# A Mamba, feed-forward, attention and expert stack: x loaded first, dt*u spread by TensorE in the first pass, new orders of work

## The chip, the cores and the metric

One core of a Trainium2 chip runs the whole program in one launch. The metric is the device time of that launch in microseconds (us). The kernel before took 1990.47 us in the median of three runs (1987.96 to 1991.94).

## What is computed

The input x has 8 items of 512 tokens by 128 features, float32. Four layers follow, each `x = layernorm(x + layer(x))`:

```python
# layer 1: two Mamba branches, forward and backward in time
xi, z = split(x @ Win); u = silu(causal_conv4(xi))       # 256 channels
dt = softplus(u @ Wx[:, :8] @ Wdt + bdt); B, C = u @ Wx[:, 8:40]   # 16 states
h = exp(dt * A) * h + (dt * u) * B ;  y = sum_s(h * C) + u * D     # over 512 steps
out = (y * silu(z)) @ Wout                                # then norms, a relu block
# layer 2: silu(x w1) * (x w2), two gelu layers of 512, w3 (ternary weights)
# layer 3: causal attention, 8 heads, 2 latent key/value heads
# layer 4: 8 experts (silu(x w1) * (x w3)) @ w2, best two, weighted by softmax
```

## The kernel before

Features lie on the 128 partitions, the 512 tokens on the free axis. The scan of layer 1 is cut into 64 **units** an item: 2 branches (d) of 2 channel halves (the four halves are hf 0 to 3), each half in 16 units of 8 channels by 16 states. For each unit n

- SyncE loads `ring[n % 6]` (L549, 512 KB): dt and dt*u of 8 channels, each repeated over 16 partitions, out of `spread_dram`, where ScalarE's queue has stored `dd` (dt and dt*u of a half, L996, semaphore `kept`);
- ScalarE takes exp(dt*A) in place (`decay`, L950);
- VectorE multiplies dt*u by B into PSUM (`drive`, L1255; B lies in `ps_brow`) and scans (`scan`, L1263) into `hst`;
- GpSimd multiplies by C into `hc` (`read_out`, L1532);
- TensorE adds up the 16 states of four units (`reduce`, L633) into `ps_y`, which VectorE gates (`gate`, L1270, L1276).

The **head** (h) makes dt, u, z, B and C of a branch: x's transposes (xT, L660), products xi, z, x and dtp (L651), the convolution (L1307), SiLUs (L981, L984) and `dt_step` (L934 to L941, L1236 to L1245). **rest** (r) is the remainder of layers 1 to 3, **experts** (x) is layer 4. They run as a pipeline over items: while item b's units run, the rest of item b-1, the experts of item b-2 and the head of item b+1 are woven in. Each engine runs its instructions in order, and the strings in `ORDER` say, for each engine, which stream takes its next step (u, r, x, h, g; VectorE takes two u steps for a unit, a product and a scan). So there are a first pass (units of item 0, order `TURN_ORDER`), a second (without x), five in a hardware loop, one more, and then what is left of rest and experts. TensorE's results go to four PSUM banks g0 to g3, given out by `place` to the least recently used; a `claim` waits until the bank's last reader is done.

In the first pass TensorE also transposes the raw weights (stream t, `turn_weights`): 20 turns, two of A before the head, then w1, w2, four each of h1 and h2, w3, wq and so on. They use g0 and g1 and the heads of this pass g2 and g3; VectorE copies every turn out (`turned_out`, L1222, semaphore `w_cp`). SyncE first raises every semaphore of `PER` by a start value, then issues 20 loads (`w_in`), x of item 0, and 37 later loads (`w_later`), the experts' weights last.

## Time and profile before

| | us |
|---|---|
| median of 3 runs | 1990.47 (1987.96 to 1991.94) |
| the profiled execution | 1983.65 |
| its span | 1981.8 |
| busy: TensorE (matmul) | 1660.5 (84%) |
| busy: VectorE | 1547.1 (78%) |
| busy: ScalarE | 1120.8 (57%) |
| busy: GpSimd | 754.8 (38%) |

In the rows PE is TensorE's matmuls, PEld its weight loads, DVE VectorE, ACT ScalarE, POOL GpSimd, SP SyncE; SPq and ACTq are instructions that issue a DMA. L549 is line 549 of the kernel. PEclk is the granted clock of TensorE as a share of 2.4 GHz (0.50 is the level of 1.2 GHz). A time in brackets is how long the engine had stood idle before an instruction, with what ended the wait. Durations are from one profiled execution.

### The profile page before, as it was taken

What the parts mean: (1) busy time and instruction counts of PE and PEld (TensorE: products, weight loads), DVE (VectorE), ACT (ScalarE), POOL (GpSimd) and SP (SyncE); (2) the same over time, 40 slices, a digit from 0 to 9 for tenths busy, and PEclk for the clock granted to TensorE, in tenths of its full rate; (3) what the DMA queues carried; (4) which work ended last, traced back from release to release, by engine and by line L of the source; (5) the groups of instructions that cost most, each with busy time, mean ns of one, the idle gap of its engine ahead of it and who ended that gap; (6) DMA issues with size and microseconds to landing.
All of it is one profiled execution on the core that took longest, in us unless ns stands there. A gap on an engine that the chain in (4) does not pass through costs nothing.

```text
span 1981.8 us, 26962 instructions
## 1 busy us (share of the span) xinstructions
PE 1660.5 (84%) x8352; PEld 768.2 (39%) x8352; DVE 1547.1 (78%) x2173; ACT 1120.8 (57%) x1555; POOL 754.8 (38%) x601
## 2 busy tenths in 40 slices
PE   2434487889997999889997899889998999989988
PEld 0210123344443445344443345344443445434545
DVE  1999899869995899769995899869996999641404
ACT  2445387358744786458744786458744785433232
POOL 0345555324533355324533355324533445310102
PEclk8655699899999999899999999999999999989999
DMA  7999999657955687657955787657955686500000
GB/s 197 228 221 225 227 230 210 150 135 181 230 133 141 158 216 178 156 123 183 231 131 140 159 214 181 156 126 181 232 132 141 165 209 184 130 0 0 6 1 6
DMA packets 107915, 309.48 MB, mean 156 GB/s; under 512 B 15970, under 2 KB 32244, under 8 KB 107764
## 3 DMA queue, kind: packets, MB, share of 16 engines
q1 hardware_dynamic: 93556, 279.32, 59.5%
q10 hardware_dynamic: 14208, 28.32, 4.4%
q8 instruction: 74, 1.21, 0.3%
q14 instruction: 77, 0.63, 0.1%
HBM read 287.67 MB, written 19.92 MB: 155 GB/s over the span
## 4 chain that ended last, share of the span: by engine, by line
PE 36%; DVE 21%; ACT 21%; issue 12%; DMA 5%; ACTq 2%; DVEq 1%; SPq 1%; POOL 0%; POOLq 0%
PE ps_pair L698 8%; PE ps_pair L795 7%; DVE sb_hst L1263 7%; ACT L919 6%; PE ps_pair L854 5%; DMA sb_ring<-spread_dram 5%; PE ps_pair L783 4%; PE ps_pair L874 3%; PE ps_pair L651 3%; ACT sb_ring L950 3%; ACT sb_mix L1099 3%; DVE sb_dd L1241 2%; DVE ps_in L1255 2%; DVE sb_nmax L1404 2%; PE ps_pair L798 2%
## 5 line engine op out<-in xcount | busy, mean ns | idle before, releaser
L1532 POOL TENSOR_TENSOR sb_hc<-sb_hst,sb_crep 128x512 f32<-128x512 f32 x512 | 659.3, 1294 | 990.0 <-DVE sb_hst L1263 617.1
L1263 DVE TENSOR_TENSOR_SCAN sb_hst<-sb_ring,ps_in 128x512 f32<-128x512 f32 x512 | 620.5, 1212 | 21.2 <-ACT sb_ring L950 13.2
L950 ACT ACTIVATE sb_ring<-sb_ring,sb_A 128x512 f32<-128x512 f32 x512 | 345.2, 713 | 227.0 <-DMA sb_ring<-spread_dram 99.5
L1255 DVE TENSOR_TENSOR ps_in<-sb_ring,ps_brow 128x512 f32<-128x512 f32 x512 | 354.3, 692 | 22.1 <-DMA sb_ring<-spread_dram 4.7
L854 PE MATMUL ps_pair<-sb_mix,sb_ew 128*128 128x512 f32 x512 | 251.3, 625 | 19.8 <-ACT sb_h L1065 9.4
L919 ACT ACT_TABLE_LOAD x193 | 247.6, 1283 | 7.3 <-DVE sb_xd L1314 3.2
L633 PE MATMUL ps_y<-sb_hc,sb_const 128*32 128x512 f32 x1024 | 154.2, 677 | 83.0 <-POOL sb_hc L1532 59.4
L795 PE MATMUL ps_pair<-sb_g,sb_h 128*128 128x512 f32 x320 | 170.5, 658 | 23.4 <-DVE sb_dd L1243 11.1
L783 PE MATMUL ps_pair<-sb_h,sb_g 128*128 128x512 f32 (+3 forms) x512 | 165.4, 452 | 6.5 <-DVE sb_nmax L1404 3.2
L854 PEld LDWEIGHTS ps_pair<-sb_mix,sb_ew 128*128 128x128 f32 x512 | 96.0, 198 | 156.7 <-issue 87.1
L874 PEld LDWEIGHTS ps_pair<-sb_ew,sb_eh 128*128 128x128 f32 x1024 | 120.6, 192 | 37.3 <-issue 13.6
L874 PE MATMUL ps_pair<-sb_ew,sb_eh 128*128 128x128 f32 x1024 | 125.1, 277 | 8.9 <-DVE sb_eh L1472 5.3
L1565 POOL TENSOR_TENSOR sb_mix<-sb_mix 128x512 f32<-128x512 f32 x56 | 71.3, 1273 | 116.4 <-DVE sb_mix L1480 116.4
L698 PE MATMUL ps_pair<-sb_g,sb_h2T 128*128 128x512 f32 x256 | 113.8, 598 | 1.8 <-ACT sb_g L1065 1.8
L1404 DVE TENSOR_REDUCE sb_nmax<-ps_pair 128x2 f32<-128x256 f32 (+3 forms) x128 | 103.0, 814 | 15.7 <-PE ps_pair L786 15.3
L698 PE MATMUL ps_pair<-sb_h,sb_h1T 128*128 128x512 f32 x256 | 113.8, 598 | 0.0
L1099 ACT ACTIVATE sb_mix<-ps_pair 128x1024 f32<-128x1024 f32 x56 | 57.0, 1018 | 80.9 <-PE ps_pair L802 52.7
L1472 DVE TENSOR_TENSOR sb_eh<-ps_pair,sb_ea 128x512 f32<-128x512 f32 x128 | 82.5, 680 | 24.6 <-PE ps_pair L854 23.1
L783 PEld LDWEIGHTS ps_pair<-sb_h,sb_g 128*128 128x128 f32 x512 | 82.4, 190 | 47.6 <-issue 17.0
L795 PEld LDWEIGHTS ps_pair<-sb_g,sb_h 128*128 128x128 f32 x320 | 57.7, 201 | 103.9 <-issue 47.5
L1133 ACT ACTIVATE sb_ea<-ps_pair 128x512 f32<-128x512 f32 x128 | 71.0, 597 | 43.1 <-PE ps_pair L854 32.1
L1480 DVE TENSOR_TENSOR sb_mix<-ps_pair,sb_gates 128x512 f32<-128x512 f32 x64 | 43.6, 681 | 59.0 <-PE ps_pair L874 58.9
(219 smaller groups left out, 2037.9 us busy)
## 6 DMA issues: line engine op xcount, KB each, us to landing
sb_ring<-spread_dram SPq DMA_DIRECT2D x512, 512.0 KB, 5.6
spread_dram<-sb_dd ACTq DMA_DIRECT2D x32, 512.0 KB, 3.0
sb_brep<-cut_dram ACTq DMA_DIRECT2D x16, 256.0 KB, 3.8
sb_crep<-cut_dram ACTq DMA_DIRECT2D x16, 256.0 KB, 4.2
sb_xtok<-in_L_attn_x_dram SPq DMA_DIRECT2D x8, 256.0 KB, 5.1
sb_ew<-in_L_ffn_w_dram SPq DMA_DIRECT2D x2, 1024.0 KB, 8.5
out_dram<-sb_yy ACTq DMA_DIRECT2D x8, 256.0 KB, 2.3
sb_h<-in_L_ffn_h_w_dram SPq DMA_DIRECT2D x1, 1024.0 KB, 7.0
```

The lines of the kernel that those rows point to most:

```text
L633: ins = pe.matmul(ps_y[32 * q:32 * q + 32, :], red, hc[:, (4 * k + q) % 6, :], start=(j == 0), stop=(j == 3))
L698: ins = pe.matmul(o[:], l, r, start=(i == 0), stop=(i == len(lhs) - 1))
L783: pe.matmul(ps_pair[i % 2][:, k, 0:(t + 1) * P], qT[:, tl, r, :], kz[:, 2 * k + hf, 0:(t + 1) * P], start=True, stop=False)
L795: pe.matmul(ps_pair[0][:, hf, :], kz[:, 2 * k + hf, j * P:(j + 1) * P], qT[:, TILES[hf].index(t), :, :], start=True, stop=False)
L854: ins = pe.matmul(o[:], l, r, start=(i == 0), stop=(i == len(lhs) - 1))
L874: ins = pe.matmul(o[:, n * D:(n + 1) * D], eh[:, e % 2, c, n * P:(n + 1) * P], ew2[:, e, c, :], start=(c == 0), stop=(c == 1))
L919: act.preload_act_table_set(name)
L950: act.activation(ring[:, n % RING, 0, :], ring[:, n % RING, 0, :], ACT.Exp, scale=A[d][:, g:g + 1]).then_inc(sem["dA"], 1)
L1255: dve.tensor_tensor(ps_in[n % 2][:], ring[:, n % RING, 1, :], ps_brow[:], ALU.mult).then_inc(sem["dbu"], 1)
L1263: dve.tensor_tensor_scan(hst[:, HST_SLOT[n], :], ring[:, n % RING, 0, :], ps_in[n % 2][:], 0.0, ALU.mult, ALU.add).then_inc(sem["scan"], 1)
L1404: dve.tensor_reduce(nmax[:, tl, r, :, hf], ps_pair[i % 2][:, :, 0:(t + 1) * P], AX.X, ALU.max, negate=True).then_inc(sem["smax"], 1)
L1532: pool.tensor_tensor(hc[:, n % 6, :], hst[:, HST_SLOT[n], :], crep[n // NU][:], ALU.mult).then_inc(sem["hc"], 1)
```

## The change

- SyncE issues x first, then 12 loads of what the first head needs (the backward branch's vectors but alog are moved behind, 9 loads, `w_one`), then raises the semaphores, then 26 later loads. The experts' weights and the router's (11 loads, `w_experts`) are issued in the second pass, one behind every fourth unit.
- A new constant `sel` (0 and 1, 128x512) is loaded. In the first pass ScalarE copies dt*u of each half to `duk`, and TensorE spreads it: for each unit one product of a 32-row slice of `sel` with `duk` into one of g0 to g3 (stream d, 64 steps). VectorE's `drive` reads dt*u from that bank and B from SBUF; the ring loads of this pass bring dt alone, 256 KB.
- ScalarE copies the ten turns of w1, w2, h1 and h2 (`moved`); VectorE keeps the other ten (`turned`). Heads, turns and spreads of the first pass share all four banks.
- All order strings are new, `TURN_ORDER` and `ORDER`; each has the same steps as before, but for the t and d steps of the first pass.

```diff
+    for j in range(NJ):
+        c[:, C_SEL + j * P:C_SEL + (j + 1) * P] = p[:, None] % 32 == CU * j + p[None, :] % CU
...
+    turned=10, moved=10, spread=64, copied=4,
...
+    if name[:2] == "du":
+        return "dbu", int(name[2:]) + 1
+    if name[:4] == "turn":
+        i = int(name[4:])
+        return ("moved", i - 1) if 2 <= i < 12 else ("turned", i + 1 if i < 2 else i - 9)
...
     DVE=(
-        "uxuxuuxuxxguuuuxuuuuuxrxuxurruxuuurxuhuruuuuuxxuururuhuhuruxuuxrruuhuuruuxuuuuhhrguuuuruuuuuuxuuuuuuhuuuruuuuu"
-        "ruuruxuguxuuruuxrrhruxuxuuhuhrxrhuxuruxururuhrruurrurxrrxrrurrururrhuhuuuhuruuuruurghhruuuuuuuuuururruuuuruurr"
-        "uurruhruur"),
+        "urxxuxuuxuxguuxxuuuuuuuuxxurxuuuxrurxuhurhxuuuuuurhuruuuuhrxuuuxruuururuuruuxuuhguururruuruuuuhxuuuuuhuuuuuuuu"
+        "uuhuuxhuuruugruuruxruxuxuxuhrxrhxuurxurruhrururrrurururrrxrrxrrhhuuuhrurruuuuhuruhruuuuuuuuuurrrhuuuruguuuurru"
+        "uuuruuruur"),
...
 TURN_ORDER = dict(
     PE=(
-        "ththhtutthttutuutthhhhttuthtutttuhtuuhuhhhhhuuhhuutuu"),
+        "tddddtddtuddudddtdttduhdutdddhhddtddtduddhthdudtddhdduddhddduhdhdduhtdddudtdtdhuddtdhudhdhtddddtdtduddddhutddh"
+        "ddhduuh"),
...
     DVE=(
-        "uthuuuuutuuuutuuuuthuhuthtuuuuuutuuuutuuuutguuuutuuhugtuthuuuuhuuhtuttuuuuuuutuuuhuuuuutuuuuuutuuuuuuuuuuguuhu"
-        "uuuhuuuuuuuhhuuuhuuuuuuhhuuuuuuuuuguuuhuuuuuuhuuuuuuuuuuuu"),
+        "ttuuuutuuuuuuuttuuutuuututuuuuuuuuhuutuuguuuhuhuutuuuuhuuguuuuuuhuuuhutuuuuuuuuuuuuuuhuuuuuuuuuuthguuuutuuuuuu"
+        "uhtuhhuuuhtuuuuuuhutuuuuuuutuuguthuuuuuuuuuuhuuuuhuuuuhuhu"),
...
 NONE = {f"g{i}": None for i in range(4)}
-PROLOGUE, _after = place(section("h" * len(ZERO), [(step, 0) for step in ZERO]), NONE, PAIRS[1])
-FIRST, _after = place(section(TURN_ORDER["PE"]), _after, PAIRS[1])
+PROLOGUE, _after = place(section("tt" + "h" * len(ZERO), [(step, 0) for step in ZERO], TURNS), NONE)
+FIRST, _after = place(section(TURN_ORDER["PE"]), _after)
 SECOND, _after = place(section(without(ORDER["PE"], "x")), later(_after))
...
+        sel = xn[:].rearrange("p (j n) -> p j n", j=NJ)
+        duk = ea[:, 2:4, :]
...
+        MOVED = ("w1", "w2", "h1", "h2")
...
-        M_LOADS, R_LOADS = 20, 37
+        M_LOADS, ONE_LOADS, R_LOADS, EXPERT_LOADS = 12, 9, 26, 3 + E
...
-            loads = [(const[:], a["const"][:, 0:C_MASK]), (mask, a["const"][:, C_MASK:C_END])]
+            loads = [(const[:], a["const"][:, 0:C_MASK])]
+            loads += [(alog[d], a[f"{pre}_Alog"].rearrange("(g c) s -> g (c s)", c=CU)) for d, pre in enumerate(("fw", "bw"))]
+            ones = [(mask, a["const"][:, C_MASK:C_SEL])]
             for d, pre in enumerate(("fw", "bw")):
-                loads += [
+                (loads, ones)[d].extend([
                     (winx[d][:], a[f"{pre}_Win"][:, 0:DI]),
                     (taps[d][:], a[f"{pre}_convw"].rearrange("(h p) k -> p h k", p=P)),
                     (winz[d][:], a[f"{pre}_Win"][:, DI:2 * DI]),
                     (wx[d][:], a[f"{pre}_Wx"].rearrange("(h p) k -> p h k", p=P)),
+                    *((cols[d][:, i, :], a[f"{pre}_{v}"].rearrange("(h p) -> p h", p=P))
+                      for i, v in enumerate(("convb", "D"))),
                     (wdt[64 * d:64 * d + R, :], a[f"{pre}_Wdt"]),
-                    (wdt[64 * d + R + 2 * S:64 * d + R + 2 * S + 1, :], a[f"{pre}_bdt"].rearrange("(o c) -> o c", o=1)),
-                    (alog[d], a[f"{pre}_Alog"].rearrange("(g c) s -> g (c s)", c=CU))]
-                loads += [(cols[d][:, i, :], a[f"{pre}_{v}"].rearrange("(h p) -> p h", p=P))
-                          for i, v in enumerate(("convb", "D"))]
-            assert len(loads) == M_LOADS, len(loads)
+                    (wdt[64 * d + R + 2 * S:64 * d + R + 2 * S + 1, :], a[f"{pre}_bdt"].rearrange("(o c) -> o c", o=1))])
+            loads += [(sel, a["const"][:, C_SEL:C_END].rearrange("p (j n) -> p j n", j=NJ))]
+            assert len(loads) == M_LOADS and len(ones) == ONE_LOADS, (len(loads), len(ones))
             later = [(wout[d][:], a[f"{pre}_Wout"].rearrange("(h p) n -> p h n", p=P))
...
-            assert len(later) == R_LOADS, len(later)
-            for name in PER:
-                sp.sem_inc(sem[name], first(name))
+            later += [(s3, a["w3_s"].partition_broadcast(P))]
+            experts = [(ew1[:], a["ew1"].rearrange("e p h -> p e h")),
+                       (ew3[:], a["ew3"].rearrange("e p h -> p e h")), (wgate[:], a["w_gate"])]
+            experts += [(ew2[:, e, :, :], a["ew2"][e].rearrange("(c p) n -> p c n", p=P)) for e in range(E)]
+            assert len(later) == R_LOADS and len(experts) == EXPERT_LOADS, (len(later), len(experts))
             with nc.allow_non_contiguous_dma(reason="per-channel vectors, once"):
+                sp.dma_start(xtok[:], a["x"][0:1].rearrange("o (n p) d -> p (o n) d", p=P)).then_inc(sem["x_in"], 16)
+                for dst, src in loads[:-3]:
+                    sp.dma_start(dst, src).then_inc(w_in, 16)
                 sp.wait_ge(w_zero, 1)
-                for dst, src in loads:
+                for dst, src in loads[-3:]:
                     sp.dma_start(dst, src).then_inc(w_in, 16)
-                sp.dma_start(xtok[:], a["x"][0:1].rearrange("o (n p) d -> p (o n) d", p=P)).then_inc(sem["x_in"], 16)
+                for name in PER:
+                    sp.sem_inc(sem[name], first(name))
+                for dst, src in ones:
+                    sp.dma_start(dst, src).then_inc(w_one, 16)
                 for dst, src in later:
                     sp.dma_start(dst, src).then_inc(w_later, 16)
 
-            def sequence(at, nxt, x_next=None):
+            def sequence(at, nxt, x_next=None, half=False, experts=()):
...
                     rows = spread[hf, 32 * q + CU * j:32 * q + CU * (j + 1), :]
-                    sp.dma_start(ring[:, n % RING, :, :].rearrange("p a t -> p (a t)"),
-                                 rows.unsqueeze(0).broadcast_to([S, CU, 2 * T])
-                                 ).then_inc(sem[f"ring{n % RING}"], 16)
+                    if half:
+                        sp.dma_start(ring[:, n % RING, 0, :], rows[:, 0:T].unsqueeze(0).broadcast_to([S, CU, T])
+                                     ).then_inc(sem[f"ring{n % RING}"], 16)
+                    else:
+                        sp.dma_start(ring[:, n % RING, :, :].rearrange("p a t -> p (a t)"),
+                                     rows.unsqueeze(0).broadcast_to([S, CU, 2 * T])
+                                     ).then_inc(sem[f"ring{n % RING}"], 16)
 
                 for n in range(UNITS):
                     load(at(0), n)
+                    if n % 4 == 3:
+                        for dst, src in itertools.islice(more, 1):
+                            sp.dma_start(dst, src).then_inc(w_experts, 16)
                     if n == 2 and nxt:
                         sp.wait_ge(sem["full_h"], at(0)("full_h", HEAD_INDEX["xT"] + 1))
                         sp.dma_start(xtok[:], x_next.rearrange("o (n p) d -> p (o n) d", p=P)).then_inc(sem["x_in"], 16)
 
-            sequence(counts(0), True, a["x"][1:2])
-            sequence(counts(1), True, a["x"][2:3])
...
-            def turn_weights():
+            def turn_weights(tabs):
                 for i, (kind, c) in enumerate(TURNED):
-                  o = turn_banks[i % 2]
+                  o = claim_of(counts(0), tabs[i >= 2])(f"turn{i}")
                   if i == 2:
                       pe.wait_ge(w_later, 16 * R_LOADS)
-                  if i >= 2:
-                      pe.wait_ge(w_cp, i - 1)
+                      pe.wait_ge(sem["turned"], 2 + first("turned"))
+                  if i == 12:
+                      pe.wait_ge(sem["moved"], 10 + first("moved"))
...
                 ins.then_inc(sem["y_red"], 1)
+
+            def spreads(at, tab):
+                row, claim = at(0), claim_of(at, tab)
+                for n in range(UNITS):
+                    hf, j, q = n // 16, n % 16 // 4, n % 4
+                    o = claim(f"du{n}")
+                    pe.wait_ge(sem["copied"], row("copied", hf + 1))
+                    rows = slice(32 * q, 32 * q + 32)
+                    pe.matmul(o[:], sel[rows, j, :], duk[rows, hf % 2, :], start=True, stop=True).then_inc(sem["spread"], 1)
+                    yield
 
...
+            pe.wait_ge(w_set, 1)
+            at, turning = counts(0), turn_weights((PROLOGUE, FIRST))
             next(turning)
             next(turning)
             alone(head(at, 0, 0, PROLOGUE))
-            interleave(TURN_ORDER["PE"], dict(u=units(at, False), t=turning, h=heads(at, FIRST)))
+            pe.wait_ge(w_one, 16 * ONE_LOADS)
+            interleave(TURN_ORDER["PE"], dict(u=units(at, False), d=spreads(at, FIRST), t=turning, h=heads(at, FIRST)))
             at = counts(1)
+            pe.wait_ge(w_mask, 1)
...
 
+            def turned_out():
+                for i, (kind, c) in enumerate(TURNED):
+                    if kind in MOVED:
+                        dst = dict(w1=w1T[:], w2=w2T[:], h1=h1T[:, c, :], h2=h2T[:, c, :])[kind]
+                        act.wait_ge(w_tp, i + 1)
+                        act.activation(dst, bank[FIRST[f"turn{i}"][0][0]][:], ACT.Copy).then_inc(sem["moved"], 1)
+                    if i >= 2:
+                        yield
...
+                    if keep:
+                        act.wait_ge(sem["spread"], row("spread", 16 * hf - 16 if hf >= 2 else 0))
+                        act.activation(duk[:, hf % 2, :], dd[:, 1, :], ACT.Copy).then_inc(sem["copied"], 1)
...
             at = counts(0)
-            alone(head(at, 0, 0, PROLOGUE))
-            interleave(TURN_ORDER["ACT"], dict(u=units(at), h=heads(at, FIRST, False)))
+            alone(head(at, 0, 0, PROLOGUE, keep=True))
+            act.wait_ge(w_one, 16 * ONE_LOADS)
+            interleave(TURN_ORDER["ACT"], dict(u=units(at), t=turned_out(), h=heads(at, FIRST, False, keep=True)))
             at = counts(1)
...
+            dve.memset(vertex[:], -0.75 * THIRD).then_inc(w_const, 1)
             dve.wait_ge(w_in, 16 * M_LOADS)
             dve.tensor_copy(identb[:], ident)
-            dve.tensor_copy(maskb[:], mask)
-            dve.tensor_copy(pick[:], const[:, C_PICK:C_PICK + 2 * KV]).then_inc(w_set, 1)
+            dve.tensor_copy(pick[:], const[:, C_PICK:C_PICK + 2 * KV])
 
...
+                    if kind in MOVED:
+                        yield
+                        continue
...
 
-            def drive(row, n):
+            def drive(row, n, tab=None):
                 if n % NU == 0:
                     dve.wait_ge(sem["brep"], row("brep", 16 * (n // NU + 1)))
                     dve.wait_ge(sem["dbu"], row("dbu", n))
-                    dve.tensor_copy(ps_brow[:], brep[:]).then_inc(sem["brow"], 1)
+                    dve.tensor_copy(eh[:, 1, 0, :] if tab else ps_brow[:], brep[:]).then_inc(sem["brow"], 1)
                     dve.wait_ge(sem["brow"], row("brow", n // NU + 1))
+                brow = eh[:, 1, 0, :] if tab else ps_brow[:]
                 dve.wait_ge(sem["scan"], row("scan", n - 1))
-                dve.wait_ge(sem[f"ring{n % RING}"], row(f"ring{n % RING}", 16 * (n // RING + 1)))
-                dve.tensor_tensor(ps_in[n % 2][:], ring[:, n % RING, 1, :], ps_brow[:], ALU.mult
-                                  ).then_inc(sem["dbu"], 1)
+                if tab:
+                    dve.wait_ge(sem["spread"], row("spread", n + 1))
+                    du = bank[tab[f"du{n}"][0][0]][:]
+                else:
+                    dve.wait_ge(sem[f"ring{n % RING}"], row(f"ring{n % RING}", 16 * (n // RING + 1)))
+                    du = ring[:, n % RING, 1, :]
...
             next(turning)
             alone(head(at, 0, 0, PROLOGUE))
-            interleave(TURN_ORDER["DVE"], dict(u=units(at, False), g=gates_of(at, False), t=turning, h=heads(at, FIRST)))
+            dve.wait_ge(w_one, 16 * ONE_LOADS)
+            dve.tensor_copy(maskb[:], mask).then_inc(w_mask, 1)
+            interleave(TURN_ORDER["DVE"], dict(u=units(at, False, FIRST), g=gates_of(at, False), t=turning, h=heads(at, FIRST)))
```

## Rows read from the trace of the kernel before

**Rows 1.** Busy times of the start and of passes (windows, us from the start).

```profile
core 0: us, PE busy (x) PEld busy (x) DVE busy (x) ACT busy (x) POOL busy (x), PEclk, DMA share, GB/s
0.00:55.66 55.66, 15.58 (x29) 6.07 (x30) 11.30 (x27) 15.29 (x22) 1.97 (x9) 0.82 0.73 201
55.66:221.56 165.90, 68.02 (x245) 22.77 (x243) 159.15 (x214) 69.88 (x102) 79.65 (x62) 0.56 0.93 224
221.56:425.25 203.69, 163.05 (x828) 67.35 (x828) 170.40 (x214) 119.56 (x167) 86.08 (x67) 0.92 0.79 188
...
648.10:871.85 223.75, 203.15 (x1031) 94.17 (x1030) 190.63 (x265) 142.82 (x197) 94.07 (x74) 0.97 0.70 168
```

**Rows 2.** Instructions in order of time, first loads to x's transposes (start, us, engine, line).

```profile
5.83 2.05 SPq L528 DMA_DIRECT2D sb_const<-in_const_dram  x1
...
15.91 0.46 SPq L528 DMA_DIRECT2D sb_cols<-in_L_attn_bw_D_dram  x1
16.42 0.47 SPq L529 DMA_DIRECT2D sb_xtok<-in_L_attn_x_dram  x1
...
18.04 0.23 DVE L1176 CAST sb_identb<-sb_const 128x128 bf16<-128x128 f32 x1 [17.07 <-DMA sb_cols<-in_L_attn_bw_D_dram]
...
19.50 1.11 PE L660 MATMUL ps_pair<-sb_const,sb_xtok 128*128 128x128 f32 x4 [0.37 <-DMA sb_xtok<-in_L_attn_x_dram]
```

**Rows 3.** The first head in order of time, and the page's row of the stores.

```profile
25.99 1.28 ACT L919 ACT_TABLE_LOAD   x1
26.00 3.37 DVE L1307 SCALAR_TENSOR_TENSOR sb_u<-ps_pair,sb_taps,sb_u 128x511 f32<-128x511 f32 x5 [0.90 <-ACT sb_u L975]
...
28.77 3.58 PE L651 MATMUL ps_pair<-sb_xT,sb_winz 128*128 128x512 f32 x4 [3.62 <-DVE sb_u L1307]
...
32.89 1.14 ACT L984 ACTIVATE sb_u<-sb_u 128x512 f32<-128x512 f32 x2
...
44.13 0.35 ACTq L996 DMA_DIRECT2D spread_dram<-sb_dd  x1
...
50.16 0.60 ACT L934 ACTIVATE sb_dd<-ps_pair 128x512 f32<-128x512 f32 x1 [8.40 <-DMA spread_dram<-sb_dd]
...
55.05 0.69 DVE L1245 TENSOR_TENSOR sb_dd<-sb_dd,sb_u 128x512 f32<-128x512 f32 x1
...
spread_dram<-sb_dd ACTq DMA_DIRECT2D x32, 512.0 KB, 3.0
```

**Rows 4.** VectorE in the first pass, one turn's copy between units, in order of time.

```profile
73.91 0.67 DVE L1222 COPY sb_h1T<-ps_pair 128x512 f32<-128x512 f32 x1
74.49 0.69 DVE L1255 TENSOR_TENSOR ps_in<-sb_ring,ps_brow 128x512 f32<-128x512 f32 x1
...
76.33 0.69 DVE L1255 TENSOR_TENSOR ps_in<-sb_ring,ps_brow 128x512 f32<-128x512 f32 x1
```

**Rows 5.** Waits of ScalarE in the first pass; VectorE's first late ring load.

```profile
ACT sb_ring L950 <- DMA sb_ring<-spread_dram: 55.4, 35, 3.5
...
222.93 0.69 DVE L1255 TENSOR_TENSOR ps_in<-sb_ring,ps_brow 128x512 f32<-128x512 f32 x1 [0.69 <-DMA sb_ring<-spread_dram]
```

**Rows 6.** One loop pass: VectorE's longest waits (648.1 to 871.9 us), and a window.

```profile
DVE sb_g L1415 <- ACT sb_rstd L1107: 7.9, 1, 7.9
...
DVE sb_yy L1415 <- ACT sb_rstd L1107: 6.5, 1, 6.5
...
720.00:732.00 12.00, 11.61 (x38) 3.92 (x36) 11.58 (x15) 7.72 (x9) 6.00 (x6) 1.00 0.87 234
```

**Rows 7.** TensorE: two products in each of two rows; windows (us, busy, PEclk, DMA share, GB/s).

```profile
21.38 3.78 PE L651 MATMUL ps_pair<-sb_xT,sb_winx 128*128 128x512 f32 x4 [0.77 <-ACT sb_xT L968]
...
679.59 1.88 PE L651 MATMUL ps_pair<-sb_xT,sb_winx 128*128 128x512 f32 x4
...
235.00:240.00 5.00, 4.18 (x9) 0.82 1.03 229
...
255.00:260.00 5.00, 2.55 (x6) 1.00 0.70 176
```

More of the change, by code:

```diff
@@ L176, with section @@
 PER["full"], PER["full_e"] = len(REST_INDEX), len(EXP_INDEX)
+TURNS = [[f"turn{i}"] for i in range(20)] + [[]]
+SPREADS = [[f"du{n}"] for n in range(UNITS)]
 CHAIN = [(step, 0) for step in ONE + [[]]] + [(step, 1) for step in ZERO]
-def section(order, heads=CHAIN):
-    steps = dict(r=iter([(step, -1) for step in REST]), x=iter([(step, -2) for step in EXPERTS]), h=iter(heads))
+def section(order, heads=CHAIN, turns=TURNS[2:]):
+    steps = dict(d=iter([(step, 0) for step in SPREADS]), t=iter([(step, 0) for step in turns]), r=iter([(step, -1) for step in REST]), x=iter([(step, -2) for step in EXPERTS]), h=iter(heads))
     uses = []
@@ L446, in two_layer_kernel @@
         block = ctx.enter_context(nc.Block())
-        turn_banks = [bank[f"g{i}"] for i in range(2)]
         def first(name):
@@ L539, in count @@
                     return value
+                more = iter(experts)
                 def load(row, n):
@@ L557, in sequence @@
                         sp.dma_start(xtok[:], x_next.rearrange("o (n p) d -> p (o n) d", p=P)).then_inc(sem["x_in"], 16)
[L559 to L560 removed]
+            sequence(counts(0), True, a["x"][1:2], half=True)
+            sequence(counts(1), True, a["x"][2:3], experts=experts)
             with sp.Fori(0, B - 3) as b:
@@ L956, in units, with head @@
                     yield
-            def head(at, ahead, d, tab, prev=True):
+            def head(at, ahead, d, tab, prev=True, keep=False):
                 row = at(ahead)
@@ L1003, in head, with heads @@
                     yield
-            def heads(at, tab, prev=True, nxt=True):
-                yield from head(at, 0, 1, tab, prev)
+            def heads(at, tab, prev=True, nxt=True, keep=False):
+                yield from head(at, 0, 1, tab, prev, keep)
                 if prev:
@@ L1189, in turned_out @@
                 for i, (kind, c) in enumerate(TURNED):
-                    o = turn_banks[i % 2]
+                    o = bank[(PROLOGUE, FIRST)[i >= 2][f"turn{i}"][0][0]]
                     if i == 2:
```

52 lines of the change are left out of this document (25 added, 27 removed).

## The prediction

> **What bounds the kernel now.** I read the busy times of each pass first [rows 1], then the start of the run in order of time [rows 2, 3], then the first pass by engine [rows 4, 5], and last one pass of the loop [rows 6]. A pass is one item's 64 units. The reader is to see four stretches: 55.7 us up to the first unit, 165.9 us for the first pass, 203.7 us for the second, then about 223 us a pass [rows 1]. In the first pass VectorE is the bound: busy 159.2 of 165.9 us, TensorE only 68.0, at a granted clock of 0.56 (mostly the 1.2 GHz level). ScalarE waits there for ring loads (55.4 us in all [rows 5]), but VectorE itself has hardly any wait, so that those loads are in time for it; from 222.9 us on they no longer are: VectorE waits eight times for a ring load, 4.6 us in all (the first is in [rows 5]). In the loop VectorE is busy 190.6 of 223.8 us and TensorE 203.2 [rows 1]; both are nearly full until the attention rounds, in which VectorE waits 7.9 and 6.5 us for the normaliser [rows 6].
>
> The profiled execution took 1983.65 us (span 1981.8), the median of three runs is 1990.47: the sum goes against 1983.65, and 6.8 us are put on top.
>
> **Start.** SyncE raises 78 semaphores up to 5.83 us, and 20 loads go out before x [rows 2]; other engines start at about 0.8. After the change the loads go first: 2.05 us for the first, 12 more at 0.46, so the last (sel, 256 KB) is issued at about 8 us. x, of the same size, was there 3.1 us after its issue (16.42 to 19.50 [rows 2]), so the weights are in at 11.0 us; from there to x's transposes the two A turns take 1.1 us (18.04 to 19.12). Transposes at 12.1 instead of 19.50: **-7.4 us**. The increments end at about 13.5, before the semaphores are asked for that come late in the list, or cost under 1 us.
>
> The first head now has four banks. Before, z00 waited for the bank of xi00 until 28.77, so the SiLUs of z ended at 33.0 and those of u came behind them, at 32.89 to 34.03 [rows 3]. With a bank of its own z follows xi at 25.2 [rows 7], z01 is there at 28.9, ScalarE is through with it at 29.5 and with u at 30.7 (its table load ends at 27.3, the convolution at 29.4 [rows 3]): **-3.3 us**.
>
> The store of dt and dt*u took 5.96 us (44.13 to 50.1 [rows 3]), beside 7.8 MB of weights; the median of such stores is 3.0 [rows 3]. It now starts at 33.4, with 4.5 MB queued and no experts' weights behind. I take 5.0, with 3.0 and 6.0 as ends: **-1.0 us**. The second half's dt*u then ends at 44.0 instead of 55.74 [rows 3]. The 26 later loads are issued from 18 to 36 us (18.4 us before), so they are in by 39; VectorE's preparation of them (57.0 to 61.2) comes behind 44.0 and does not wait.
>
> **First pass, VectorE.** A unit costs it 1.84 us (74.49 to 76.33 [rows 4]), 118 for 64. The ten copies of w1, w2, h1, h2 go: 0.67 us each, but the next product starts 0.59 us after such a copy [rows 4], so 10 x 0.59 = 5.9; the mask's cast (0.2) comes in: **-5.7 us**. The product has one operand in PSUM and one in SBUF before and after, so it stays at 0.69.
>
> **First pass, added work.** ScalarE gets ten copies and four of dt*u at 0.60 us (as its copy of xT), 8.4 us; it is busy 69.9 of 165.9 us, so they are hidden while decays stand ahead of need. Its earliest turn copy holds a bank that du3 needs; it comes after three decays, at about 48 us, and du3 is needed at 51. TensorE gets 64 products of 32 rows by 512 columns. The nearest rows are its products of 128 and 41 rows: 1.89 us each at the 1.2 GHz level, 0.90 at 2.4 [rows 7]. So 121 or 58 us beside its 68.0 (at a clock of 0.56). Cold it would want 189 us, more than VectorE's 153.5; but where it was busy 4.18 of 5 us the clock went up, and it stayed up with 2.55 busy of 5 [rows 7]. With the products it will be busy 55 to 65% in short gaps. I take the high clock for most of the pass. What can be late: a spread product can run only three banks ahead, shared with turns and heads, and behind it in TensorE's queue stand y's reductions, each of which waits for GpSimd. For VectorE that adds between 0 and 25 us of waits; I take **+5** (nearer to nothing, since before the change VectorE stands idle 6.7 us of this pass, with a TensorE that runs cold and is as often in wait behind y's reductions [rows 1]).
>
> The Trainium skill ("TensorE: Matmul & The Clock Gate", section "A second HAM failure mode: psum-queue depth-cycling") speaks against the change: a TensorE that cycles through PSUM banks with small idles between its groups is throttled and released again and again. By it the pass would come out as in the second case below.
>
> **Ring loads.** Halved in the first pass: 256 KB against 1.85 us is 142 GB/s, where 512 KB a unit were 283, above the 229 GB/s that the queues moved when saturated [rows 7]. The ring is then full at the second pass, and the 4.6 us of waits there go. In their place come 2 MB of experts' weights behind units 3 and 7 of the second pass: 1 MB at 229 GB/s is 4.6 us each, 9 us against a cushion of about 6 units less the 0.4 us by which each full load falls behind. I put 4.6 of it as wait: net **0**, ends -4.6 and +5.
>
> **The new orders of all later passes.** This edit has no row of its own. Counted in the strings of VectorE: before, 53 of 64 units and all gates stand ahead of the dt step that frees the banks of the attention rounds; after it 51 units, and the last gate behind. That moves two units (3.7 us) and a gate (0.73 + 0.69) into the stretch where VectorE waits 14.4 us [rows 6]. If VectorE alone set the time before it, a pass would gain 5.1 us. TensorE was just as full there (in one stretch of 12 us it was busy 11.61 and VectorE 11.58 [rows 6]), so most will not pass. Against it, some steps may now be late by up to 2 us. Between -5.1 and +2 I take -1.5 for each of six passes: **-9 us**.
>
> **Sum.** -7.4 - 3.3 - 1.0 - 5.7 + 5 + 0 - 9 = -21.4: 1962.2 for a profiled execution, **1969** in the median.
>
> **The rivals.**
> 1. Forecast, within about 9 us of 1969: 0.47.
> 2. Slower: TensorE stays at 1.2 GHz in the first pass and becomes its bound. 189 us instead of 153.5 + 5: 30.5 us more, 1999.6. At the high clock its work is about 95 us, so it decides from a share f of low clock at which 189f + 95(1-f) passes 153.5, f = 0.62, and eats all of the 21.4 from 0.91. For it: the clock of 0.56 now. Against: the rise in [rows 7]. 0.08. This is the case of the page named above.
> 3. TensorE's queue order, not its clock, holds the spread products up: 20 us of waits instead of 5, 1984. 0.12.
> 4. The orders gain nothing and cost 2 us a pass: +12 instead of -9, 1990, no change: 0.10. With 3 us, +18: 1996, slower: 0.08.
> 5. The moved units pay nearly in full, -4.5 a pass, -27: 1951. For it: 14.4 us of wait to fill. 0.15.
>
> **How the numbers follow.** A measurement can tell about 0.2%, 4 us. Cases 1, 3 and 5 are faster, 0.74; the first half of case 4 is the same, 0.10; case 2 and the rest of 4 are slower, 0.16. The range leaves out the slower cases, 0.16, and the far end of case 5: 1947 to 1993. The likeliest case alone: 1960 to 1978.
>
> **What the changed profile would show.** x's transposes at about 12 us, VectorE's first unit near 49 with its second head's dt*u ended at 44; TensorE's clock in the first pass over 0.8 and no long waits of ps_in for its spread product; the second pass starting near 205 instead of 221.6; ring loads late after unit 4 of the second pass; passes of 218 to 223 us, with shorter waits for the normaliser. The prediction is wrong if the passes move by over 3 us either way, if the spread products queue behind the reductions, or if the sel load or late increments hold up the first head.

## The result, and the profile after

The changed kernel took 2008.6 us in the median (2008.1 to 2009.5) against 1989.2 for the kernel before on the same chips: a ratio of 1.0096, 95% interval 1.0079 to 1.0114. It is slower by about 19 us; the forecast was 1969, with a range of 1947 to 1993. The profiled execution has a span of 2006.4 against 1981.8.

Windows of the changed kernel, cut like [rows 1] (columns as there):

```profile
0.00:45.67 45.67, 17.17 (x33) 6.42 (x34) 15.12 (x41) 19.20 (x29) 1.97 (x9) 0.76 0.76 199
45.67:214.20 168.53, 141.75 (x368) 42.87 (x366) 150.10 (x188) 73.24 (x112) 80.04 (x62) 0.58 0.37 118
214.20:423.29 209.09, 166.63 (x828) 68.76 (x828) 170.45 (x215) 118.60 (x165) 84.80 (x67) 0.90 0.82 196
650.72:876.25 225.53, 203.91 (x1033) 94.93 (x1033) 190.92 (x266) 142.38 (x196) 93.40 (x74) 0.96 0.69 167
```

Cut at the first copy of B of each pass, the difference of the spans is accounted for like this:

| stretch | before | after | difference | forecast |
|---|---|---|---|---|
| start and first pass, to the second pass | 221.6 | 214.2 | -7.4 | -12.4 |
| second pass | 203.7 | 209.1 | +5.4 | -1.5 |
| five passes of the loop | 1110.1 | 1127.4 | +17.3 | -7.5 |
| the last pass and what is left | 446.5 | 455.7 | +9.2 | 0 |
| sum | 1981.8 | 2006.4 | +24.6 | -21.4 |

So the stretch up to the second pass still gains, and everything behind it loses. Two signs stand in the rows. In the first pass TensorE has twice the work and is still at the 1.2 GHz level (clock 0.58). In the loop the busy times are those of before [rows 1], and the pass shown is 1.8 us longer (the five together 17.3): it waits, it does not work more. The table compares two single profiled executions; that of before was 5.6 us under the median, so 24.6 us here stand beside 19 in the medians.

The waits of VectorE in one loop pass (line that waited, for what: us in total, times, longest). Before, 871.85 to 1094.24:

```profile
DVE sb_g L1415 <- ACT sb_rstd L1107: 7.9, 1, 7.9
DVE sb_yy L1415 <- ACT sb_rstd L1107: 6.4, 1, 6.4
...
DVE sb_nmax L1404 <- PE ps_pair L786: 1.2, 4, 0.3
...
DVE sb_hst L1263 <- POOL sb_hc L1532: 0.3, 1, 0.3
...
DVE sb_hst L1263 <- issue: 0.2, 1, 0.2
```

After, 876.25 to 1101.34:

```profile
...
DVE sb_yy L1478 <- ACT sb_rstd L1163: 7.3, 1, 7.3
DVE sb_hst L1326 <- issue: 3.3, 3, 1.8
DVE sb_nmax L1467 <- PE ps_pair L827: 2.6, 6, 0.9
DVE sb_hst L1326 <- POOL sb_hc L1598: 2.1, 1, 2.1
DVE sb_g L1478 <- ACT sb_rstd L1163: 1.6, 1, 1.6
```

The reader is to see that the waits for the normaliser did shrink as forecast, 14.3 to 8.9 us, and that scans now have longer waits that the profile puts down to nothing (`issue`, 3.3 instead of 0.2), scans wait for GpSimd (2.1 instead of 0.3) and maxima for TensorE (2.6 instead of 1.2). The rows below show that the longest of the `issue` waits is one for a decay.

Where the longest new wait of a scan comes from, in order of time, VectorE first, then ScalarE, in the changed kernel:

```profile
724.08 0.69 DVE L1303 TENSOR_TENSOR sb_dd<-sb_dd,sb_u 128x512 f32<-128x512 f32 x1
...
726.17 0.69 DVE L1319 TENSOR_TENSOR ps_in<-sb_ring,ps_brow 128x512 f32<-128x512 f32 x1
728.70 1.22 DVE L1326 TENSOR_TENSOR_SCAN sb_hst<-sb_ring,ps_in 128x512 f32<-128x512 f32 x1 [1.84 <-issue]
```

```profile
724.80 0.35 ACTq L1049 DMA_DIRECT2D spread_dram<-sb_dd  x1
725.34 0.57 ACTq L1056 DMA_DIRECT2D sb_brep<-cut_dram  x1
726.01 0.55 ACTq L1058 DMA_DIRECT2D sb_crep<-cut_dram  x1
726.60 1.28 ACT L963 ACT_TABLE_LOAD   x1 [2.98 <-issue]
727.89 2.56 ACT L994 ACTIVATE sb_ring<-sb_ring,sb_A 128x512 f32<-128x512 f32 x4
```

ScalarE's string has here the step `keep2` (it waits for the third half's dt*u, stores it, and loads B and C). It stands behind 22 decays; in the string of before it stands behind 24. VectorE makes that dt*u at the same point as before (its last product starts 73.4 us into the pass; 73.5 before). ScalarE therefore stands in `keep2` until 724.8, issues three DMAs, loads a table, and only then makes the decay for which the next scan waits. In the kernel before the same place has the three issues, but two decays more in hand and no table load between the issues and the next decay, and the scan does not wait:

```profile
722.32 0.35 ACTq L996 DMA_DIRECT2D spread_dram<-sb_dd  x1
...
723.69 0.69 DVE L1255 TENSOR_TENSOR ps_in<-sb_ring,ps_brow 128x512 f32<-128x512 f32 x1
724.28 1.21 DVE L1263 TENSOR_TENSOR_SCAN sb_hst<-sb_ring,ps_in 128x512 f32<-128x512 f32 x1
```

### The profile page after: what moved, and what is told of

It reads as the page before. It is cut to its first block, busy times and chain, and to the rows that moved or that the text cites. A ratio compares the mean times of both kernels' runs of the same rounds, so it can differ in the third digit from the quotient of the medians.

```text
span 2006.4 us, 27294 instructions
## 1 busy us (share of the span) xinstructions
PE 1756.6 (88%) x8480; PEld 798.6 (40%) x8480; DVE 1543.0 (77%) x2163; ACT 1126.8 (56%) x1565; POOL 750.8 (37%) x601
## 4 chain that ended last, share of the span: by engine, by line
PE 54%; ACT 15%; DVE 15%; issue 9%; POOL 3%; DMA 2%; ACTq 1%; DVEq 0%; SPq 0%; POOLq 0%
PE ps_pair L739 12%; PE ps_pair L895 8%; PE ps_pair L836 7%; PE ps_pair L824 6%; PE ps_pair L692 5%; PE ps_pair L915 5%; DVE sb_hst L1326 4%; PE ps_y L664 3%; ACT L963 3%; ACT sb_mix L1155 2%; POOL sb_hc L1598 2%; PE ps_pair L675 2%; PE ps_pair L839 2%; ACT sb_ring L994 2%; DMA sb_ring<-spread_dram 2%
## 5 line engine op out<-in xcount | busy, mean ns | idle before, releaser
L1326 DVE TENSOR_TENSOR_SCAN sb_hst<-sb_ring,ps_in 128x512 f32<-128x512 f32 x512 | 620.8, 1213 | 53.0 <-issue 21.4
L1319 DVE TENSOR_TENSOR ps_in<-sb_ring,ps_brow 128x512 f32<-128x512 f32 x448 | 310.6, 693 | 27.1 <-DMA sb_ring<-spread_dram 9.3
L895 PE MATMUL ps_pair<-sb_mix,sb_ew 128*128 128x512 f32 x512 | 260.7, 644 | 6.0 <-DVE sb_g L1415 2.1
L739 PE MATMUL ps_pair<-sb_g,sb_h2T 128*128 128x512 f32 x256 | 120.6, 622 | 0.0
L675 PE MATMUL ps_pair<-sb_ea,sb_xn 32*128 32x512 f32 x128 | 77.4, 1021 | 13.4 <-DVE sb_dd L1301 4.9
```

The lines of the kernel that those rows point to most:

```text
L675: pe.matmul(o[:], sel[rows, j, :], duk[rows, hf % 2, :], start=True, stop=True).then_inc(sem["spread"], 1)
L739: ins = pe.matmul(o[:], l, r, start=(i == 0), stop=(i == len(lhs) - 1))
L895: ins = pe.matmul(o[:], l, r, start=(i == 0), stop=(i == len(lhs) - 1))
L1319: dve.tensor_tensor(ps_in[n % 2][:], du, brow, ALU.mult).then_inc(sem["dbu"], 1)
L1326: dve.tensor_tensor_scan(hst[:, HST_SLOT[n], :], ring[:, n % RING, 0, :], ps_in[n % 2][:], 0.0, ALU.mult, ALU.add).then_inc(sem["scan"], 1)
```

## The experiments

Each was timed beside the kernel before; the ratio is to that. All compute the same as the kernel before except e5, whose text says what differs.

| run | edit | median us | ratio | 95% interval |
|---|---|---|---|---|
| e1 | changed kernel, old `ORDER` | 1983.4 | 0.9967 | 0.9948 to 0.9987 |
| e2 | kernel before, new `ORDER` | 2014.1 | 1.0126 | 1.0080 to 1.0172 |
| e4 | e1 without spreads | 1976.1 | 0.9929 | 0.9905 to 0.9953 |
| e5 | e1, spreads over 128 rows | 1975.2 | 0.9917 | 0.9885 to 0.9949 |
| e6 | e1, experts' loads in first pass | 1976.0 | 0.9941 | 0.9919 to 0.9962 |
| e7 | e5 made exact, with e6 | 1967.3 | 0.9901 | 0.9874 to 0.9927 |
| e8 | before, new ScalarE string alone | 2086.5 | 1.0511 | 1.0475 to 1.0548 |
| e9 | before, the other three new | 2079.9 | 1.0470 | 1.0451 to 1.0489 |
| e10 | changed kernel, keep2 two decays later | 1989.8 | 1.0016 | 1.0000 to 1.0031 |
| e11 | e10, GpSimd's old string | 1987.6 | 0.9988 | 0.9971 to 1.0006 |
| e12 | e4 with e6 | 1976.9 | 0.9951 | 0.9936 to 0.9966 |
| e13 | e1, keep2 two decays earlier | 1994.2 | 1.0041 | 1.0028 to 1.0055 |

**The orders against the rest: e1 and e2.** e1 puts the strings of `ORDER` of before into the changed kernel, e2 the new ones into the kernel before; `TURN_ORDER` stays as it is in each.

> The changed kernel with the ORDER strings of before (TURN_ORDER stays new). Theory A, the new strings cost the loss: five loop passes took 1127.4 us in the changed kernel against 1110.1, the last pass and the end 455.7 against 446.5, so about 26 us come back: 1982 us, loop passes of about 222.7. Theory B, something else makes the later passes longer (the banks' state handed over, the experts' loads, other addresses): 2008 us, passes of 225.5.

> The kernel before with the new ORDER strings alone. Theory A: 1989 + 26 = 2015 us, loop passes of about 225.5. Theory B: 1989 us, passes of 222.7. If the two edits act together only, e1 and e2 both stand near 1989.

Theory A holds. The same strings cost 25.2 us in one kernel (2008.6 against 1983.4) and about 25 in the other (ratio 1.0126, a wide interval of 16 to 34 us). In e1 the five loop passes take 1106.7 us and the end 446.4, before's or a little under. The second pass is no longer by the strings (210.0 in e1, 209.1 in the changed kernel): they cost 4.1 us a pass of the loop in the mean and 9 in the last pass and the end. The slowdown is the strings; all the rest of the change together gains 0.3%.

**Which step of the strings: e8, e9, e10, e13.** e8 gives the kernel before ScalarE's new string alone, e9 the three others.

> The kernel before, with only ScalarE's string of the later passes new. All new strings together cost it 25 us (e2: 2014.1), 2.7 us in each pass of the loop (225.1 against 222.4). Theory H: ScalarE's string does most of it, because it puts the step that waits for dt*u and issues the store (keep2) behind 22 decays instead of 24, while VectorE reaches that dt*u at the same unit as before; decays then come late: 224 to 225.5 us a pass and 2000 to 2014 us in all. Rival I: the loss comes from TensorE's or VectorE's string and ScalarE's alone is harmless: passes of 222 to 223 us and 1987 to 1992.

> The kernel before with the new strings of TensorE, VectorE and GpSimd, and its own old string of ScalarE; e2, with all four new, took 2014.1, and e8, with ScalarE's alone, 2086.5 (237 us a pass, the strings no longer fit each other). e10 showed that one letter of ScalarE's string is worth 19 us in the changed kernel. Theory K: ScalarE's old string, which has keep2 behind 24 decays, cures that loss here too, at 224 us a pass: 1990 to 1998. Rival L: the old string is as far from the other three new ones as in e8 and the passes run to 230 us or more: above 2020. If the three new strings are as good as I forecast (1.5 us a pass gained), it would be under 1985.

Both came out near 2080, 237 and about 235 us for a pass of the loop. e8 lies far above both of its theories; in it VectorE's scans wait 21.4 us for decays in one pass. e9 came out as its rival L had said. Each engine's string fits the other three; split, neither half can be priced, and the two runs don't say which step of the strings costs the time. e10 leaves the strings together and moves one letter of ScalarE's, `keep2`, the sixth `h` of the line:

```diff
-        "xuxxuxuxuxuuxxruruxruhuuruuxrxxhhrruuuuxruhrurruruhurhuuruxuxxruxuurhuuruuruxuuruxuuuhhxruxhrhurrxhurrxruruurh"
+        "xuxxuxuxuxuuxxruruxruhuuruuxrxxhhrruuuuxruhrurruruhuruuhruxuxxruxuurhuuruuruxuuruxuuuhhxruxhrhurrxhurrxruruurh"
```

> The changed kernel with one letter of ScalarE's string moved: keep2 (the copy and store behind the wait for dt*u) after 24 decays instead of 22, all else new. In the changed kernel VectorE's scan then waits 1.84 us for the decay behind it (728.70 us). Theory H in its narrow form (this one step is the loss): passes of 223 to 224 us instead of 225.2, seven of them: 1997 to 2001 us against 2008.6. Rival J: the 1.84 us are only where the delay shows; ScalarE and GpSimd are late in other places as well (decays behind 29 and 40, GpSimd's adds), so the pass gains under 0.6 us: 2004 to 2009.

18.8 us came back by the medians (2008.6 to 1989.8), 16 by the ratios (1.0096 to 1.0016): two thirds to three quarters of the 25, and more than theory H had said. Half a pass of the loop (first copy of B to the second) fell from 99.0 us to 97.1, before's length. ScalarE in e10 at this place:

```profile
722.00 1.28 ACT L963 ACT_TABLE_LOAD   x1
723.17 0.35 ACTq L1049 DMA_DIRECT2D spread_dram<-sb_dd  x1
723.29 0.72 ACT L994 ACTIVATE sb_ring<-sb_ring,sb_A 128x512 f32<-128x512 f32 x1
```

The table is loaded before the wait, and a decay starts 0.12 us behind the store's issue. VectorE's waits marked `issue` at scans fall from 3.3 to 1.4 us a pass; those for the normaliser, for GpSimd and of the maxima stay as in the changed kernel:

```profile
DVE sb_hst L1326 <- issue: 1.4, 2, 1.2
```

The five loop passes take 1116.9 us (1127.4 with the step early) and the end 448.4 (455.7). In the changed kernel the wait of 1.84 us stands in every one of the passes two to eight (1.84 to 1.94, 13.0 us in all); in e10 it stands in none. Of the 18.4 us between the two spans, 13.8 lie in the first halves of these passes, where the step stands. The rest lies elsewhere, and it is not even: in the third and fourth pass of the loop the second half gave the gain back (225.0 and 224.6 us in e10, 225.1 and 224.9 in the changed kernel). e13 is the reverse test, with all old strings (the fifth and sixth `h`; the step ahead of `keep2` has to go with it):

```diff
-        "uxxxxxuxuuuuxurruxuuxruhrxuurxuxhrruuxuhhxurruuruuruuhxhruururrxxuuuhruuuuruururxhhuxxxuuurhruhrurrrxxxuhuxrrr"
+        "uxxxxxuxuuuuxurruxuuxruhrxuurxuxhrruuxuhhxurruuruuhhruuxruururrxxuuuhruuuuruururxhhuxxxuuurhruhrurrrxxxuhuxrrr"
```

> e1 (all old strings, 1983.4) with two letters of ScalarE's string moved: dt2 and keep2 behind 22 decays instead of 24, everything else old. It asks whether the place of keep2 costs the time by itself, without the other new strings. Theory H: VectorE reaches this dt*u at its unit 23, as before, so ScalarE stands in keep2 until then, decay 22 comes late, and VectorE's scan waits 1.5 to 3 us in each of seven passes: passes of 224 to 225.5 instead of 222.3, 1994 to 2006 in all. Rival R: keep2's place matters only with the other new strings, whose units leave VectorE no cover; then the passes stay within 0.7 us and the run at 1981 to 1988.

Against e1, ratio to ratio, it costs 0.74%, 15 us. Half a pass grows from 97.1 to 98.4 us, the five passes from 1106.7 to 1118.2; the first halves of the seven passes hold 10.2 of the 16.7 us between the spans. ScalarE stands still for 8.4 us and the scan behind it is late (ScalarE, then VectorE):

```profile
953.46 2.56 ACT L994 ACTIVATE sb_ring<-sb_ring,sb_A 128x512 f32<-128x512 f32 x4 [8.39 <-issue]
```

```profile
954.27 1.22 DVE L1326 TENSOR_TENSOR_SCAN sb_hst<-sb_ring,ps_in 128x512 f32<-128x512 f32 x1 [0.64 <-DVE ps_in L1319]
```

The profile puts that wait down to the product, which had ended at 953.63; the first of the four decays begun at 953.46 ended about 0.5 us later (an estimate, a quarter of 2.56 us).

So the place of this one step costs 15 to 19 us in either set of strings: theory H holds, with both signs of the edit. A quarter (e10) and four tenths (e13) of the difference between the spans lie outside the halves in which the step stands, and how they come about was not traced.

**What is left of the strings' cost: e11.** It is e10 with GpSimd's string of before.

> e10 (the changed kernel with keep2 two decays later, 1989.8) with GpSimd's old string. What is left of the new orders' cost against e1 (1983.4) is 6.4 us. In each pass of e10 VectorE waits 2.1 us once for GpSimd's product (its scan at 1076.06 us), where the kernel before waits 0.3. Theory M: GpSimd's new string, with its adds in other places, is the cause: passes 1 to 2 us shorter, 1976 to 1986. Rival N: that wait is the shadow of something on TensorE's or VectorE's side, and the passes stay at 225: 1987 to 1993; if the old adds come where they hold up a product of the new order, above 1993.

The wait of 2.1 us for GpSimd's product is still there, and the five loop passes take 1116.2 us against 1116.9 in e10: theory M, 1 to 2 us a pass, falls. The median is 2 us under e10's and the two intervals overlap, so a small gain is not excluded. What e10 and e11 stand above e1, 6 and 4 us by the medians, 10 and 4 by the ratios, stays unexplained. Two places were seen and not tested. Behind the middle of a pass a scan waits 1.24 us for a decay that stands behind two table loads of ScalarE (in e10 the scan at 984.29, the loads at 979.78 and 982.18). It does so in six passes of e10, 7.4 us in all, and of e11; in e1 the waits of scans marked `issue` come to 2.4 us in the whole run. The difference of 5.0 us has the size of what is left, but no run moves those steps. And TensorE holds more of the chain that ended last. Its shares by engine in e10, then in e1 (before: PE 36%):

```profile
PE 55%; ACT 15%; DVE 14%; issue 9%; POOL 3%; DMA 2%; SPq 2%; ACTq 1%; DVEq 0%; POOLq 0%
```

```profile
PE 39%; DVE 21%; ACT 20%; issue 13%; DMA 4%; ACTq 2%; DVEq 1%; SPq 0%; POOL 0%; POOLq 0%
```

That share is a weak sign: e13, with TensorE's old string, has 48%. No run separates TensorE's string from VectorE's.

**The first pass: e4, e5.** e4 takes the spread products, their copies and the halved loads out again. e5 keeps them and lets each product run over all 128 rows instead of 32; dt*u of the first item is then a sum over four rows, another number than the reference's, and the loads, decays and instruction counts are the same.

```diff
-                    rows = slice(32 * q, 32 * q + 32)
+                    rows = slice(0, P)
```

> As e1, but without TensorE's spread products, duk copies and halved ring loads: the first pass loads dt*u with the ring as before; early loads, four banks and ScalarE's copies of the turns stay. Theory C, the 32-row products at the low clock cost VectorE its gain (18.4 us of idle time in the first pass against 6.7 before): the first pass shrinks from 168.5 to about 160 us, 1974 us. Theory D, the idle time comes from the weave of heads and turns in TURN_ORDER, not from the products: 168 us, 1982 us.

> As e1, but each spread product takes all 128 rows of sel and duk instead of 32 (so it adds up four channel groups and dt*u is another number; the rest is computed as before). The instruction count and columns are the same. Theory E, the clock stayed at the 1.2 GHz level through stretches of 5.00 of 5 us busy because only 32 rows of the array worked: the granted clock of the first pass goes from 0.58 to over 0.8, products take about 0.9 us, VectorE's waits for them go, 5 to 8 us faster than e1. Theory F, the rows do not matter: clock 0.58, same time as e1.

Windows of the first pass: e1, e4, e5.

```profile
45.95:214.47 168.52, 141.88 (x368) 42.86 (x366) 150.09 (x189) 73.41 (x112) 79.97 (x62) 0.58 0.39 119
```

```profile
45.74:207.63 161.89, 64.53 (x238) 21.72 (x238) 148.78 (x188) 75.24 (x113) 79.72 (x62) 0.61 0.96 230
```

```profile
46.01:205.44 159.43, 117.16 (x368) 38.75 (x366) 150.09 (x188) 73.47 (x112) 80.04 (x62) 0.87 0.41 125
```

Theories C and E hold. With 32 rows the pass takes 168.5 us, 6.6 more than without spreads at all; with 128 rows the same 368 instructions run at a clock of 0.87 and it takes 159.4. VectorE stands idle for 18.4 us of the pass in e1 and for 9.3 in e5. Only a part of that is the wait for the spread product itself: 4.2 us in six waits in e1 and in the changed kernel, 1.7 us in e5. The rest is spread over other waits: 3.9 us of the convolution's step for ScalarE (1.3 in e5), 2.5 of a scan for GpSimd (the same in e5) and smaller ones. That TensorE was not idle in the slow case shows in the changed kernel:

```profile
95.00:100.00 5.00, 5.00 (x11) 1.71 (x8) 4.91 (x7) 2.44 (x5) 3.73 (x4) 0.50 0.38 107
100.00:105.00 5.00, 5.00 (x12) 0.70 (x10) 4.03 (x7) 4.10 (x7) 1.94 (x2) 0.50 0.42 106
```

By the records it is busy in every microsecond from 90 to 120 us, and at the 1.2 GHz level throughout; the ends of products are modelled, so this says only that its records leave no gap.

**The second pass: e6.** The experts' 11 loads move into the first pass, whose queues are two thirds empty (DMA share 0.37).

```diff
-            sequence(counts(0), True, a["x"][1:2], half=True)
-            sequence(counts(1), True, a["x"][2:3], experts=experts)
+            sequence(counts(0), True, a["x"][1:2], half=True, experts=experts)
+            sequence(counts(1), True, a["x"][2:3])
```

> Same as e1 (changed kernel with the old order of the later passes), but the experts' 11 loads are issued in the first pass, behind every fourth unit, and none in the second. In e1 the second pass took 210.0 us (214.5 to 424.4) against 203.7 of the kernel before. Theory F: the two loads of 1 MB behind units 3 and 7 of the second pass make its ring late and cost it about 6 us; then the second pass here takes 203 to 206 us, and the run is 4 to 7 us under e1's 1983.4: 1976 to 1979. The DMA share of the first pass was 0.37 in e1, so that 4 MB more there cost nothing. Rival G: the second pass is longer because its start finds less work ahead (the first pass leaves VectorE without lead); then it stays at 209 to 211 us and the run at 1982 to 1985. If the loads now disturb the first pass (168.5 us in e1), it gets longer by up to 4 us.

The second pass took 202.6 us instead of 210.0, the first 2.0 more. Theory F holds. VectorE's waits for ring loads in it were 9.3 us in the changed kernel and 7.1 in e1, and 1.5 in e6. Two of those in the changed kernel stand behind the two loads of 1 MB (in order of time):

```profile
229.28 0.70 DVE L1319 TENSOR_TENSOR ps_in<-sb_ring,ps_brow 128x512 f32<-128x512 f32 x1 [4.51 <-DMA sb_ring<-spread_dram]
...
242.17 0.70 DVE L1319 TENSOR_TENSOR ps_in<-sb_ring,ps_brow 128x512 f32<-128x512 f32 x1 [2.62 <-DMA sb_ring<-spread_dram]
```

**A version that beats both: e7, and what the spreads are worth: e12.** e7 makes e5 exact. Sixteen 0/1 matrices of 128x128, zero outside the unit's 32 rows, lie in the room of the experts' first weights until those are loaded, behind unit 15 of the second pass; the other experts' loads go into the first pass.

```diff
+    for q in range(4):
+        for j in range(NJ):
+            s = C_SEL + (4 * q + j) * P
+            c[:, s:s + P] = p[:, None] == 32 * q + CU * j + p[None, :] % CU
...
-                    rows = slice(32 * q, 32 * q + 32)
-                    pe.matmul(o[:], sel[rows, j, :], duk[rows, hf % 2, :], start=True, stop=True).then_inc(sem["spread"], 1)
+                    pe.matmul(o[:], sel[:, 4 * q + j, :], duk[:, hf % 2, :], start=True, stop=True).then_inc(sem["spread"], 1)
```

> e1 with each spread as a product of all 128 rows: sixteen 0/1 matrices of 128x128, zero outside the 32 rows of the unit's channels, in the room of the experts' first weights; those are loaded late in the second pass (behind unit 15), the others in the first pass. What is computed is the same. In e5, where 128 rows worked but summed a wrong dt*u, the granted clock of the first pass rose from 0.59 and 0.57 to 0.93 and 0.82 and the pass took 159.4 us instead of 168.5. Theory E (the clock goes by how many rows work) with theory F (the two big loads early in the second pass cost 6 us): first pass 159 to 161 us, clock above 0.8, second pass 203 to 206 us, the run 1966 to 1971. If zeros in most rows count as not working, the clock stays near 0.58, the first pass takes 168, and the run 1975 to 1979. If F is wrong, it is 1973 to 1976 with the high clock. The 1 MB selection load comes before the second unit and may delay the first ones by up to 4 us.

> e4 (old orders, no spread products, full ring loads in the first pass) with the experts' loads in the first pass as in e6. It prices what the spreads make room for. In e4 the first pass took 161.9 us at a DMA share of 1.00 and 0.92, so there is no room: 4 MB at the 229 GB/s of full queues are 18 us. Theory P: VectorE then waits for ring loads, the first pass grows by 10 to 18 us to 172 to 180, the second shrinks by 6 to 7 to 204: 1979 to 1988. Rival Q: the ring of six units and the slower start give enough cover, and the first pass grows by under 5 us: 1969 to 1975, as good as e7 (1967.3), and then the spread products bring nothing.

e7's first and second pass, then e12's first:

```profile
45.19:206.76 161.57, 116.97 (x371) 39.43 (x369) 149.86 (x189) 74.51 (x114) 79.71 (x62) 0.88 0.47 140
206.76:409.86 203.10, 162.34 (x823) 67.48 (x828) 170.36 (x215) 118.63 (x166) 85.39 (x67) 0.93 0.79 191
```

```profile
45.75:215.37 169.62, 64.67 (x238) 21.68 (x238) 148.99 (x188) 74.35 (x111) 79.72 (x62) 0.60 0.97 236
```

e7 takes 1967.3 us, 1.0% less than before. Most of the 128 rows meet zeros here, and the granted clock is that of e5 (0.88). e12 lies between its two theories: full queues cost the first pass 7.7 us (VectorE's waits for ring loads rise from 5.2 to 10.1), not 10 to 18, and the run is 9.6 us behind e7. With the clock up and the room in the queues unused the spreads bring nothing that can be measured (e5 1975.2, e4 1976.1). So they do pay, once the clock is up and something else uses the room that they leave in the queues.

## Why the prediction was wrong

**The orders were the largest miss.** In the profiled executions 46 us lie between the forecast of -21.4 and the measured +24.6. 34.0 of them are in the five loop passes, the last pass and the end, where the only term was "Between -5.1 and +2 I take -1.5 for each of six passes". The other 12 came up to the end of the second pass, from the first pass and the ring loads. The terms follow in the order of the sum.

**Start: right, and a little under.** Two instructions of the changed kernel's start, in order of time:

```profile
0.76 0.46 SPq L541 DMA_DIRECT2D sb_xtok<-in_L_attn_x_dram  x1
...
10.26 1.11 PE L701 MATMUL ps_pair<-sb_const,sb_xtok 128*128 128x128 f32 x4
```

x's transposes came at 10.26 us (forecast 12.1); the first issue took 0.46 us, not the 2.05 that I had carried over from [rows 2]. The store took 3.4 us, not 5.0, and the second dt*u ended at 41.42, not 44.0: -14.3 instead of -11.7. The first unit began only 10.0 us earlier, because VectorE's preparation of the later loads now stands ahead of it (the mask's cast up to the copy of B, 4.3 us); before it stood behind the first product. Before, then after:

```profile
55.66 0.69 DVE L1251 COPY ps_brow<-sb_brep 128x512 f32<-128x512 f32 x1
...
56.98 0.29 DVE L1194 COPY sb_wkrep<-sb_wkd 128x64 f32<-128x64 f32 x2
```

```profile
41.34 0.22 DVE L1569 CAST sb_maskb<-sb_eh 128x128 bf16<-128x128 f32 x1
...
45.67 0.43 DVE L1309 COPY sb_eh<-sb_brep 128x512 f32<-128x512 f32 x1
```

**First pass: the place of the error was named, its size not.** VectorE fell to 150.1 us busy; with the 4.3 us that moved ahead of the pass that is 154.4, where 153.5 were forecast. But it stood idle for 18.4 us (6.7 before); the term of +5 was about 12. The step that failed is "I take the high clock for most of the pass": the granted clock was 0.58. It read the clock by the busy share in [rows 7], from products that were nearly all of 128 rows, and applied it to products of 32. e5 and e7 show that at the same instruction count the pass has 0.58 with 32 rows and 0.87 and 0.88 with 128. With the clock up, in e5, VectorE's idle time is 2.6 us over that of before, inside what the term allowed. The second rival's clock was right, its price not: TensorE's busy time in the pass grew by 73.7 us (77.4 against e4), not 121, and the spreads cost the pass 6.6 us (e1 against e4), not 30.5. The third rival, 20 us of waits by TensorE's order of work, is near the 18.4 in size and not the cause: e5 has the same order and half of that idle time. The Trainium skill ("TensorE: Matmul & The Clock Gate", section "What's actually happening") says that the gate goes by how busy the engine has been, and the section weighed in the prediction ties the throttling to small idles between groups. The trace doesn't agree with either: the clock is 0.50 where the records show 5.00 of 5 us busy. The line in the prediction that has the second pass start "near 205" also disagreed with its own sum, which gave 209, and the share of 0.91 in rival 2 comes out as 0.90.

**Ring loads: sized wrong.** Net 0 had ends of -4.6 and +5; measured +4.6 in waits (9.3 against 4.7) and, by e6, 7.4 us of the pass. I had charged a 1 MB load with its own 4.6 us and set six units of cushion against it; behind the first one alone VectorE waited 4.5 us, although the ring was full by my reckoning.

**The new orders: the sign was wrong.** Forecast -9, measured +25. The gain that I argued is there: the waits for the normaliser fell by 5.4 us where I had said 5.1. It was given back, and more. The step of the prediction that failed is the upper end, "some steps may now be late by up to 2 us": it was taken from no row, and I had counted only VectorE's string. What was missed is a wait in ScalarE's: `keep2` waits on VectorE, and with two decays fewer ahead of it its wait, three issues and a table load (724.8 to 727.9) stand between VectorE and its next decay. Its place is worth 15 to 19 of the 25 us (e10, e13); what costs the rest stays open. Rival 4's second half had the sign and nearly the size, 3 us a pass, but it named no step. The strings cost nothing in the second pass, 4.1 us in the mean of the five loop passes (1127.4 against 1106.7 in e1), and 9.3 in the last pass and the end, for which I had no term.

## What to carry to other kernels

When the order of an engine's work changes, list for every step that waits on another engine how much work of this engine lies finished ahead of it, before and after; a step that moved by two small instructions was worth 15 to 19 us of 2000 here. Price a change by stages, and test the orders apart from the rest: the rest of this change gained 0.3%, and 1.0% once two of its parts were put right. A new burden on TensorE should be costed at the clock which such products get. And room made in a DMA queue should be used: here it brought nothing that could be measured until the experts' loads were moved into it, and about 10 us then (e7 against e12).
